# A four-layer graph network on one core: split edge transfers, earlier weights and statistics, one-hots three groups ahead, 64 tiles of picks

## The reference, cut to what matters

```python
def _bn(x, gamma, beta):                       # over all nodes, for each feature
    m = jnp.mean(x, axis=0)
    v = jnp.mean((x - m) ** 2, axis=0)
    return gamma * (x - m) * jax.lax.rsqrt(v + EPS) + beta

def _hconv(x, src, dst, ew, w1, b1, w2, b2, g, b):
    h = jax.nn.relu(x @ w1 + b1)
    msg = ew[:, None] * h[src]
    agg = jax.ops.segment_sum(msg, dst, num_segments=x.shape[0])
    h = agg @ w2 + b2
    return jax.nn.relu(_bn(h, g, b))
...
# layer 3: h = _hconv(...); h = relu(_bn(h, bn1)); the same once more without the last relu; then
# a mixture of 16 experts, each node by its 2 best, hidden width 512
```

## Time and profile before

| | us |
|---|---|
| median of three timed runs | 7885.76 (7880.52 to 7893.24) |
| the profiled execution | 7827.13 |
| its span | 7825.40 |
| TensorE busy in it | 5375.0 |
| VectorE busy | 4168.1 |
| GpSimd busy | 3553.2 |
| ScalarE busy | 2370.7 |

### The profile page before, as it was taken

How to read it: one execution, slowest core, us unless ns; L and a number is a source line. 1 busy time by engine, 2 the same in 40 slices (tenths; PEclk the granted TensorE clock), 3 DMA queues, 4 the chain that set the end, 5 groups by cost and what they waited for, 6 DMA issues and landing times. The chain is left out here.

```text
span 7825.4 us, 86636 instructions
## 1 busy us (share of the span) xinstructions
PE 5375.0 (69%) x22652; PEld 3704.3 (47%) x22653; DVE 4168.1 (53%) x11843; ACT 2370.7 (30%) x4657; POOL 3553.2 (45%) x3101
## 2 busy tenths in 40 slices
PE   2886477777639866769797667639995454554585
PEld 1554356566526644446454455525663333332374
DVE  9102488888853367764455677782224344333544
ACT  1222344444302223322112555542331221121132
POOL 4777677777560257750001454500005772776043
PEclk9999677777759988889798677768997767666687
DMA  2444333333230265550001222200003332333323
GB/s 53 118 118 95 92 112 111 108 110 110 75 95 30 49 126 163 159 142 1 8 10 33 68 71 67 69 6 13 13 8 89 93 88 59 91 91 87 95 81 102
DMA packets 392190, 607.94 MB, mean 78 GB/s; under 512 B 158638, under 2 KB 276444, under 8 KB 390890
## 3 DMA queue, kind: packets, MB, share of 16 engines
q0 software_dynamic: 174592, 350.59, 17.4%
q1 hardware_dynamic: 216990, 247.74, 11.0%
q10 hardware_dynamic: 308, 6.40, 0.3%
HBM read 458.94 MB, written 144.63 MB: 77 GB/s over the span
## 5 line engine op out<-in xcount | busy, mean ns | idle before, releaser
L779 POOL DMA_INDIRECT conv_rows<-rows_b,index x832 | 849.6, 1021 | 1286.8 <-SPq L2560 949.7
L811 DVE TENSOR_TENSOR acc<-acc,ps 125x257 f32 (+1 forms) x1664 | 701.6, 422 | 952.1 <-DMA mpnn_edge<-records_src 325.9
L2606 PE MATMUL ps<-conv_rows,conv_weight_of 128*125 128x256 f32 x1664 | 619.4, 514 | 620.1 <-issue 292.7
L332 POOL DMA_INDIRECT records_src<-by_src_edge_stage,by_src_edge_slot x400 | 562.5, 1406 | 498.7 <-DMA by_src_edge_stage<-edge_rows 378.6
L2606 PEld LDWEIGHTS ps<-conv_rows,conv_weight_of 128*125 128x125 f32 x1664 | 365.4, 246 | 874.1 <-issue 559.3
L779 POOL DMA_INDIRECT mpnn_rows<-rows_b,index x416 | 480.0, 1154 | 321.4 <-POOLq L1615 124.1
L496 POOL DMA_INDIRECT records_dst<-front_back,front_dst_addr x400 | 503.2, 1258 | 260.2 <-issue 260.2
L779 POOL DMA_INDIRECT gat_rows<-rows,index x416 | 500.9, 1204 | 259.5 <-PE ps L1089 138.7
L779 POOL DMA_INDIRECT hyp_rows<-rows,index x416 | 416.6, 1002 | 407.8 <-PE ps L2208 273.9
L1417 PE MATMUL ps<-room,experts_w 128*128 128x500 f32 (+1 forms) x1344 | 547.8, 545 | 64.8 <-DMA experts_w<-in_L_ffn_w 40.2
L1576 ACT ACTIVATE experts_hid<-ps,experts_consts 128x500 f32<-128x500 f32 (+1 forms) x448 | 302.4, 678 | 937.3 <-PE ps L1417 830.4
(11 more groups left out here) (572 smaller groups left out, 10616.1 us busy)
## 6 DMA issues: line engine op xcount, KB each, us to landing
mpnn_edge<-records_src SPq DMA_DIRECT2D x104, 512.0 KB
edge_rows<-front_edge_ring SPq DMA_DIRECT2D x100, 503.9 KB
by_src_edge_stage<-edge_rows SPq DMA_DIRECT2D x100, 503.9 KB
conv_rows<-rows_b,index POOLq DMA_INDIRECT x832
front_attr<-in_edge_attr SPq DMA_DIRECT2D x100, 125.0 KB
rows_b<-acc SPq DMA_DIRECT2D x15, 560.0 KB
second_w<-in_L_ffn_w SPq DMA_DIRECT2D x1, 8192.0 KB
gat_rows<-rows,index POOLq DMA_INDIRECT x416
```

Of the source, the lines that this page charges most:

```text
L332: pool.indirect_dma_start(out=self.S.records["src"], out_offset=bass.IndirectOffsetOnAxis(ap=self.addr[:, c:c + 1], axis=0), in_=self.stag ...
L779: pool.indirect_dma_start(out=rows[:, n % U, t, :], out_offset=None, in_=table, in_offset=bass.IndirectOffsetOnAxis(ap=ends[:, n * G + t:n ...
L811: dve.tensor_tensor(here, here, S.ps[0:P, t % banks, 0:width], ALU.add).then_inc(added, 1)
L2606: pe.matmul(S.ps[0:P, t, 0:D], weight_of[:, q.slot, t, :], rows[:, q.slot, t, :], start=True, stop=True).then_inc(summed, 1)
```

## The change

It does seven things. (1) The loads of attributes and the stores of `edge_rows` in the front use `move_rows`, two DMAs of 13 and 112 rows in place of one of 125, and so do the loads in `EdgeScatter.load`. (2) Both convolutions' weights are loaded during the layer norm ln6, ahead of them, into buffers of their own. (3) The statistics of the first normalisation of each convolution are taken chunk by chunk beside the products. (4) Those of the second are taken for the first half as soon as ScalarE has applied that half. (5) In the sums VectorE accumulates group q - 3 behind the select of group q, in place of group q - 1. (6) PICK_TILES is 64 in place of 68. (7) The gate's weights, loaded in ln6 before too, now come behind the six loads of the convolutions.

```diff
@@ EdgeScatter.load
-            sp.dma_start(self.stage[:, r], view[:, k * SG:(k + 1) * SG, :]).then_inc(self.loaded[r], 16)
+            move_rows(sp, self.stage[:, r], view[:, k * SG:(k + 1) * SG, :], self.loaded[r])
@@ EdgeScatter.scatter
-                pool.wait_ge(self.loaded[r], 16 * (k // self.RING + 1))
+                pool.wait_ge(self.loaded[r], ROWS_IN * (k // self.RING + 1))
@@ front, queue of SP
                 for g in range(AR):
-                    sp.dma_start(attr[:, g], attributes[:, g * AG:(g + 1) * AG, :]).then_inc(attr_in[g], 16)
+                    move_rows(sp, attr[:, g], attributes[:, g * AG:(g + 1) * AG, :], attr_in[g])
 ...
                 for g in range(AGROUPS):
                     if g + AR < AGROUPS:
                         sp.wait_ge(attr_turned, g + 1)
-                        sp.dma_start(attr[:, g % AR], attributes[:, (g + AR) * AG:(g + AR + 1) * AG, :])\
-                            .then_inc(attr_in[g % AR], 16)
+                        move_rows(sp, attr[:, g % AR], attributes[:, (g + AR) * AG:(g + AR + 1) * AG, :],
+                                  attr_in[g % AR])
                     sp.wait_ge(edge_out, 3 * (g + 1))
-                    sp.dma_start(out[:, g * AG:(g + 1) * AG, :], ring[:, g % ER]).then_inc(rows_stored[g % ER], 16)
+                    move_rows(sp, out[:, g * AG:(g + 1) * AG, :], ring[:, g % ER], rows_stored[g % ER])
 ...
-                    sp.wait_ge(rows_stored[r], 16 * len(range(r, AGROUPS, ER)))
+                    sp.wait_ge(rows_stored[r], ROWS_IN * len(range(r, AGROUPS, ER)))
 
@@ front, TensorE
-                        pe.wait_ge(attr_in[g % AR], 16 * (g // AR + 1))
+                        pe.wait_ge(attr_in[g % AR], ROWS_IN * (g // AR + 1))
@@ front, ScalarE
                     if g >= 1:
                         h = g - 1
                         if h >= ER:
-                            act.wait_ge(rows_stored[h % ER], 16 * (h // ER))
+                            act.wait_ge(rows_stored[h % ER], ROWS_IN * (h // ER))
@@ column_norm
-def column_norm(ch, dve, src, stats, mv, sem_ask, sem_done, count, eps, gamma, beta, tmp, affine):
-
-
-    for k in range(K):
-        for c in range(NCHUNK):
-            at = CH * c * P
-            width = len(chunk_blocks(c)) * P
-            ch.step(dve.bn_stats(stats[:, k, c, :], src[:, k, at:at + width]))
+def chunk_statistics(ch, dve, src, stats, k, c):
+    at = CH * c * P
+    width = len(chunk_blocks(c)) * P
+    ch.step(dve.bn_stats(stats[:, k, c, :], src[:, k, at:at + width]))
+
+
+def column_norm(ch, dve, stats, mv, sem_ask, sem_done, count, eps, gamma, beta, tmp, affine):
+
@@ hyperconv
-def hyperconv(nc, S, A, n, hT):
+def hyperconv(nc, S, A, n, hT, weights, loaded):
 
 
     ends, local, blk = S.end["dst"], S.local["dst"], S.blk["dst"]
     col = lambda v: S.pcol[:, S.column[f"L3_gnn_{v}"]:S.column[f"L3_gnn_{v}"] + K]
     source = S.xT if n == 1 else hT
     with phase(nc, f"conv{n}") as (sb, sem):
-        w1, w2, b1 = sb("w1", [128, K, D]), sb("w2", [128, K, D]), sb("b1", [P, D])
-        loaded, dve_step, product, out, stored = (
-            sem(x) for x in ("loaded", "dve_step", "product", "out", "stored"))
+        w1, w2, b1 = weights[n - 1]
+        dve_step, product, out, stored = (sem(x) for x in ("dve_step", "product", "out", "stored"))
         ch = Chain(None, dve_step)
         with nc.Block() as block:
             @block.sync
             def _(sp):
-                for dst, v in ((w1, "w1"), (w2, "w2")):
-                    sp.dma_start(dst[:], A[f"L3_gnn_c{n}_{v}"].rearrange("(k p) f -> p k f", p=128)).then_inc(loaded, 16)
-                sp.dma_start(b1[:], row(A[f"L3_gnn_c{n}_b1"])).then_inc(loaded, 16)
-                sp.wait_ge(loaded, 48)
                 move_rows_behind(sp, S.rows_b.rearrange("(t p) c -> p t c", p=P), S.acc[:, :, 0:D], stored, out)
                 sp.wait_ge(stored, NB // LEAD * ROWS_IN)
 
             @block.tensor
             def _(pe):
-                pe.wait_ge(loaded, 48)
+                pe.wait_ge(loaded, 96)
@@ hyperconv, first block, VectorE
-                dve.wait_ge(loaded, 48)
+                dve.wait_ge(loaded, 96)
@@ hyperconv, second block, VectorE
-                pipeline(dve, (0, select), (1, lambda q: accumulate(dve, S, q, ids, D, 8, summed, added)),
+                pipeline(dve, (0, select), (3, lambda q: accumulate(dve, S, q, ids, D, 8, summed, added)),
                          written_out=True)
 
@@ hyperconv, last block, VectorE
                     dve.wait_ge(product2, m + 1)
                     dve.tensor_scalar(hT[:, f, at:at + width], S.ps[:, 4 + m % 4, 0:width],
                                       col(f"c{n}_b2")[:, f:f + 1], None, ALU.add).then_inc(out2, 1)
-                dve.wait_ge(out2, NCHUNK * K)
+                    for old in (m - 1,) if m < NCHUNK * K - 1 else (m - 1, m):
+                        if old >= 0:
+                            dve.wait_ge(out2, old + 1)
+                            chunk_statistics(ch, dve, hT, stats, old % K, old // K)
                 for a, v in enumerate((f"c{n}_", f"bn{n}_")):
-                    if a:
-                        dve.wait_ge(applied, 2)
-                    column_norm(ch, dve, hT, stats, mv, ask, root, a + 1, EPS, col(v + "g"), col(v + "b"),
+                    for k in range(K if a else 0):
+                        dve.wait_ge(applied, k + 1)
+                        for c in range(NCHUNK):
+                            chunk_statistics(ch, dve, hT, stats, k, c)
+                    column_norm(ch, dve, stats, mv, ask, root, a + 1, EPS, col(v + "g"), col(v + "b"),
                                 tmp, affine[:, a])
@@ hypergraph
-def hypergraph(nc, S, A):
+def hypergraph(nc, S, A, gate_weights):
+
     with phase(nc, "hgraph") as (sb, sem):
         hT = sb("hT", [128, K, N])
-        hyperconv(nc, S, A, 1, hT)
-        hyperconv(nc, S, A, 2, hT)
+        loaded = sem("loaded")
+        weights = [(sb(f"w1_{n}", [128, K, D]), sb(f"w2_{n}", [128, K, D]), sb(f"b1_{n}", [P, D])) for n in (1, 2)]
+
+        def all_weights(sp):
+            for n, (w1, w2, b1) in zip((1, 2), weights):
+                for dst, v in ((w1, "w1"), (w2, "w2")):
+                    sp.dma_start(dst[:], A[f"L3_gnn_c{n}_{v}"].rearrange("(k p) f -> p k f", p=128)).then_inc(loaded, 16)
+                sp.dma_start(b1[:], row(A[f"L3_gnn_c{n}_b1"])).then_inc(loaded, 16)
+            gate_weights(sp)
+
+        layer_norm(nc, S, "ln6", early_stats=S.acc[:, :, D:D + 6], on_sync=all_weights)
+        hyperconv(nc, S, A, 1, hT, weights, loaded)
+        hyperconv(nc, S, A, 2, hT, weights, loaded)
 
 
 NE3 = 16
 F3 = 512
-PICK_TILES = (2 * N + NE3 * 127) // 128 + 1
-PICK_TILES += -PICK_TILES % U
+PICK_TILES = (2 * N + NE3 * 127) // 128
+assert PICK_TILES % U == 0
 
 
 def sort_picks(nc, S, key, expert_of, node_of, pick_of, begin):
@@ convolutions_and_mixture
-        layer_norm(nc, S, "ln6", early_stats=S.acc[:, :, D:D + 6], on_sync=gate_weights)
-        hypergraph(nc, S, A)
+        hypergraph(nc, S, A, gate_weights)
         ffn3(nc, S, A, out, gates)
```

## The result

The changed kernel took 7781.18 us (7774.60 to 7787.10, four runs), the kernel before 7883.14 (7871.01 to 7893.24, four runs): a ratio of 0.9871 with a 95% interval of 0.9854 to 0.9888, or 102 us less (88 to 115).

A forecast was written before the change was run, and what follows sets the result against it. No engine bounds the whole; GpSimd's scatter chain sets the front, and it has the largest share in the sums, TensorE in the picks. Terms sum to -80.5 us, from 7885.8 to 7805, range 7755 to 7849 (8 in 10).

The forecast's parts named there:

- C: Rival, convolutions' sums: earlier selects remove GpSimd's full-ring pauses; half is -43 us (7762), all -86 (7724); chance 0.15.
- Front: Front's edge loop: split transfers shorten eight GpSimd pauses from 6.6 to about 3.5 us; -25 us (0 to -34).
- the bound of 2.40: Front: the -34 us limit, with all eight GpSimd pauses at 2.40 us, a pause seen beside little traffic.
- The same bytes lie on all: Front: a 125-row transfer loads about five of 16 engines; split, its bytes spread over all.
- Norm and routing blocks: Blocks after the attention: split loads land sooner; norm -3 us (0 to -6), routing -6 (-3 to -7).
- Weights early: Convolutions' start: first products no longer wait for loads; -4.8 us each, -9.6 together (-8 to -10).
- Statistics: Convolutions' normalisations: -5.4 us for the first set and 2.9 saved on the second, -16.6 for both convolutions (-14 to -17).
- Three groups ahead: Convolutions' sums: GpSimd's pauses stay, only the end shortens; -5 us for both (-86 to +12).
- the tail: Sums, 25.5 us behind the last gather: three selects done earlier, -2.4 to -3.6 us a convolution.
- Picks: Picks: four fewer steps of 3.68 us are -14.8, with less sorting -15.3 us.
- B: Rival: GpSimd's pauses are its own and splits give nothing anywhere; -46.5 us in all, 7839; chance 0.22.
- D: Rival, front's loop: SyncE's issues double to 7.2 us a group and bound the front; +64 us, 7950; chance 0.07.

The follow-up runs named there:

- before_again: The kernel before, unchanged, run once more for a second profile on a chip of the fast kind: 7492.39 us.
- splits_only: The kernel before with all three kinds of transfers split and nothing else of the change: 7450.39 us, ratio 0.9946 to the kernel before.
- lag_1_again: The kernel after with the sums again one group behind the selects, on a slow-kind chip: 7732.48 us, ratio 0.9891 to the kernel before.

## Why the prediction was right, point by point

**The whole.** Forecast 7805 (7755 to 7849), measured 7781. The term-by-term sum was -80.5; the change brought -102 (88 to 115), -85 (79 to 102) and -90 (81 to 107) on three chips, and its two halves measured apart -81. The measured time lies inside the wide range, but below the 7785 that the prediction gave as the end of its likeliest case's own range. That narrow range doesn't follow from its terms either: front 0 to -34 and timing by 5 around 7805 give 7791 to 7835. And C's 7762 keeps the lag's -5, which its 7724 leaves out; without it half of C is 7767. Of the 20 us by which the first chip's value exceeds the sum nothing was traced to a stage.

**Front: -25 forecast, -29 measured** (806.1 to 777.3; -33 on the chip of before_again, 810.0 to 777.2). The step was right: the loop's 80 us gained nothing, GpSimd's chain ended the front, and its pauses shrank when the stores were cut at row 112. The eight averaged 6.43 before, a little under the 6.6 of the prediction's sum, and fell to 2.75 (2.30 to 3.70), not 3.5: three of them are below the bound of 2.40 (2.30, 2.30 and 2.36) although the loop has more traffic than the place that it was read from, the others 2.6 to 3.7. "The same bytes lie on all" was right too, but it holds for the stores alone; splitting the attributes' loads was worth nothing once the stores were split. What GpSimd does in a pause stays open. It comes every 39 scatters (62 us apart after, 64 before) and is longer when whole transfers of 125 rows, or of 115, are in flight. A fetch of its next instructions would fit the fixed count, but of the packets that the profile lists under its two instruction queues none falls into the eight pauses of before or of after, and in the other runs one to three do.

**Norm and routing blocks: -3 and -6 forecast, -9.8 measured together** (286.1 to 276.3). The split was otherwise than forecast. In the norm block the first load lands 2.8 us sooner (from issue at 2137.92 to 2143.14, 5.2 us, where it took 8.0), and that buys nothing. GpSimd and VectorE in after:

```profile
2143.14 5.80 POOL L332 DMA_INDIRECT records_src<-by_src_edge_stage,by_src_edge_slot  x1 [63.39 <-DMA by_src_edge_stage<-edge_rows]
2149.24 11.41 POOL L332 DMA_INDIRECT records_src<-by_src_edge_stage,by_src_edge_slot  x1 [0.30 <-issue]
2160.96 6.54 POOL L332 DMA_INDIRECT records_src<-by_src_edge_stage,by_src_edge_slot  x1 [0.30 <-issue]
```

```profile
2147.91 11.68 DVE L1155 TENSOR_TENSOR room<-room,acc 125x6400 f32<-125x6400 f32 x1
2159.62 6.82 DVE L1156 TENSOR_TENSOR room<-room,attention_gat_bias 125x6400 f32<-125x6400 f32 x1
```

A scatter that takes 1.19 us when nothing holds it takes 11.41 and 6.54 here, and each ends 1.1 us behind one of VectorE's two long additions (11.68 and 6.82). In the kernel before two scatters do the same, at 2148.54 and 2160.25 (11.40 and 6.55), so an earlier start only makes the first scatter wait 5.80 in place of 2.97. The Trainium skill, page "SBUF — State Buffer", section "Who interferes with whom", says that a VectorE instruction with two inputs in SBUF contends with a GpSimd instruction that reads there, through a shared port that one holds for its whole instruction; this trace agrees, and VectorE's addition had started first each time. From the first load's issue to the last scatter's end the block took 79.2 us before and 77.7 after: -1.5. The routing block took 96.3 (2244.04 to 2340.38) and takes 88.5 (2243.52 to 2332.02): -7.8 where -6 was forecast. The first load lands only 1.7 us sooner (5.6 in place of 7.3 from its issue), half of what was taken for it. Most of the rest are three waits for later loads (2.21, 1.64 and 1.73 us) and two of 0.67 and 0.77, which are gone.

**Weights early: -4.8 each forecast, -4.6 measured for conv1** (21.8 to 17.2 us). For conv2 the stage holds the statistics too: -13.5 together. How that divides wasn't measured.

**Statistics: -8.3 each forecast, -9.0 measured behind conv2**, and -8.7 in front of conv2's products if the weights' share there is the forecast's 4.8.

**Three groups ahead: -5 forecast, -6 to +1 measured, not told from nothing.** What the prediction said against C was right: GpSimd waits for sums, these wait for VectorE's adds, and the lag doesn't change how many there are; the pauses stayed (conv1's gathers took 604 us after, where 593 were forecast). Its own term for the lag, the tail, was wrong. It took 25.5 us and three selects behind the last gather for the rule. In before two selects and 29 adds stood there, because VectorE had been held shortly before and was held for 9.7 us more. With one group behind, the tail of the slow kind's profiles goes from 13.0 to 25.3 us and holds none to two selects; on the fast kind it is 13.4 to 15.4 with one group and 14.3 to 15.2 with three, with no select in it either way. So where nothing holds VectorE there is nothing for the lag to take, and the fall from 25 to 14 us in the first pair of profiles, which looks like the forecast coming true, was in great part where the last bout of held adds fell. The prediction also left open why the ring fills; the holds of VectorE above are what the traces show.

**Picks: -15.3 forecast, -15.7 measured** (247.1 to 231.4).

**Rivals.** B, the split changes nothing, fell with splits_only and with the pauses. The sentence "Don't bother" of the Trainium skill (page "DMA: Bandwidth & Descriptors", section "Rules for kernel authors") doesn't hold here: it advises a single transfer of 128 partitions, and the single one here has 125 rows. C, the lag removes the full ring, fell with lag_1_again: the ring is full as often. D, SyncE becomes the bound, fell by the issue times: four issues take 2.0 us where two took 3.6, and splitting either transfer shortened the other's issues, so their length was waiting, as argued against it.

## What to carry to other kernels

Count how a transfer's rows divide before counting its bytes: 516 KB in one DMA of 125 rows held up its own loop, the loads behind it and the GpSimd chain beside it, and 112 + 13 rows removed it where 115 + 10 did next to nothing. A loop that gets 80 us faster is worth what the engine that ends the stage gets out of it, here 29. When a ring is full, follow the waits to the engine that empties it before pricing the pause, and don't take a tail of one profile for the rule. And work of an engine that ends two short blocks, but idles in the long one behind them, is best moved there (the two blocks took 31 us less here).

## What the runs showed of the hardware

In the front's loop an issue on SyncE took 0.30 to 0.35 us at the median with the stores split (0.96 for the larger part of a load when the loads were split too), and 1.5 to 2.1 us with whole transfers of 125 rows; splitting either transfer shortened the other's issues (2.06 to 0.32 us, 1.55 to 0.26 us). GpSimd's scatters stood through whole VectorE additions, up to 11.41 us for one of 1.19. And the same program differed by 4 to 5% between chips (7488 to 7883 us), nearly all of it in the stages with gathers: messages 582 against 677 us, a convolution's sums 553 against 618, the attention 1210 against 1254. In the sums the difference goes with adds of VectorE that are held for up to 5.2 us while their input lies ready, 253 to 294 us of them against none.
